# A graph network's sums over incoming edges: one product of 96 columns and one of 48 in place of three of 48

## The reference

```python
def _L0(x, w, b, src, dst, val):                  # sums to dst, once
    return relu(segment_sum(val[:, None] * (x @ w)[src], dst) + b)
def _L1(h, src, dst, ...):                        # sums to src, once
    msg = gate * h[dst] * (cw * mj)[:, None]
    agg = segment_sum(msg, src); tot = segment_sum(mj, src)
def _L2(x, w, src, dst):                          # twice
    x = segment_sum(x[src] * w[:, None], dst)
def _L3(x, src, dst, weight, bias):               # three times (Chebyshev, K = 4)
    prop = lambda h: segment_sum(w[:, None] * h[src], dst)
```

## Time and profile before

| | us |
|---|---|
| median of three runs | 18501.3 (18497.01 to 18546.9) |
| span of the profiled execution, first to last instruction | 16154.8 |
| what lies around the span, median less span | 2346.5 |
| seven stretches of the sums, together | 3718 |
| mean granted TensorE clock over the span | 0.809 |

### The profile page before, as it was taken

The page is one execution under the profiler, slowest core; times in us unless marked ns, Lnnn a source line. Parts: engine busy times, 40 slices in busy tenths (PEclk is TensorE's granted clock), DMA queues, the critical chain, the costliest instruction groups (busy, mean ns, idle before and its releaser), DMA issues. The chain is left out here.

```text
span 16154.8 us, 581780 instructions
## 1 busy us (share of the span) xinstructions
PE 10820.7 (67%) x194032; PEld 8866.5 (55%) x194033; DVE 12006.3 (74%) x25806; ACT 7455.3 (46%) x21241; POOL 7887.2 (49%) x7665
## 2 busy tenths in 40 slices
PE   5676767667610487867776677777766686676678
PEld 4555555555510366745555565656655565565556
DVE  9666766666633587789996888788777778777776
ACT  0111211112222366844456565766664474475466
POOL 0577777777767666013330077047307605713730
PEclk8777776776755699988888889998997797698789
DMA  8344433333367698979988698989779898988987
GB/s 341 111 124 124 124 120 124 124 122 123 123 167 186 177 371 308 321 261 342 331 298 257 231 350 295 304 310 350 272 252 385 317 313 334 369 281 310 386 288 237
DMA packets 1719187, 4103.16 MB, mean 254 GB/s; under 512 B 336706, under 2 KB 625440, under 8 KB 1718294
## 3 DMA queue, kind: packets, MB, share of 16 engines
q1 hardware_dynamic: 1287670, 3065.78, 57.5%
q0 software_dynamic: 431248, 1034.11, 16.6%
q10 hardware_dynamic: 144, 1.60, 0.0%
HBM read 2932.16 MB, written 1702.21 MB: 287 GB/s over the span
## 5 line engine op out<-in xcount | busy, mean ns | idle before, releaser
L1399 POOL DMA_INDIRECT messages<-exp_stage,exp_block_rows x3324 | 3569.8, 1074 | 4376.1 <-ACT exp_stage L1379 1827.6
L845 POOL DMA_INDIRECT records<-rec,row_i x3125 | 3116.6, 997 | 1442.7 <-issue 816.2
L1540 PEld LDWEIGHTS sum_sums<-sum_slots,sum_onehot 128*128 128x128 bf16 x93072 | 2522.1, 96 | 1138.7 <-issue 1131.8
L1540 PE MATMUL sum_sums<-sum_slots,sum_onehot 128*128 128x48 bf16 (+1 forms) x93072 | 2677.7, 183 | 637.5 <-DVE h L1466 507.1
L1497 ACT ACTIVATE sum_onehot<-iota_b,sum_late_places 128x128 bf16<-128x128 bf16 x5817 | 1910.2, 391 | 770.7 <-PE sum_sums L1540 687.8
L1257 PE MATMUL exp_rows<-tab,h 128*128 x39888 | 1806.2, 197 | 521.1 <-DVE h L1298 219.1
L1263 PE MATMUL exp_rows<-tab,h 128*128 x13296 | 1437.6, 284 | 923.5 <-ACT exp_stage L1379 668.0
L1257 PEld LDWEIGHTS exp_rows<-tab,h 128*128 128x128 bf16 x39888 | 1565.3, 102 | 876.5 <-issue 731.5
L1263 PEld LDWEIGHTS exp_rows<-tab,h 128*128 128x128 bf16 x13296 | 1222.1, 126 | 1138.7 <-issue 1106.5
L668 ACT COPY rec<-emeta 128x40 f32 (+1 forms) x625 | 140.2, 224 | 3070.9 <-DMA records<-rec,row_i 3070.9
L1298 DVE TENSOR_SCALAR h<-exp_places,pcol 128x2048 bf16<-128x2048 bf16 x1662 | 1271.9, 765 | 170.1 <-DMA exp_places<-src_places 146.5
(11 more groups left out here) (301 smaller groups left out, 22101.0 us busy)
## 6 DMA issues: line engine op xcount, KB each, us to landing
sum_slots<-messages SPq DMA_DIRECT2D x1662, 576.0 KB, 5.3
exp_places<-src_places SPq DMA_DIRECT2D x1662, 512.0 KB
sum_slots<-messages SPq DMA_DIRECT2D x277, 600.0 KB, 5.4
messages<-zeros SPq DMA_DIRECT2D x124, 1149.0 KB
l_places<-dst_places SPq DMA_DIRECT2D x277, 512.0 KB, 6.4
recc<-records SPq DMA_DIRECT2D x277, 448.0 KB, 4.7
l_gate<-records SPq DMA_DIRECT2D x277, 448.0 KB
records<-fill SPq DMA_DIRECT2D x215, 576.0 KB, 12.8
```

What stands on the lines that cost most here:

```text
L845: pool.indirect_dma_start(rec_dram, bass.IndirectOffsetOnAxis(ap=row_i[:, g, k:k + 1], axis=0), rec[:, g, k, :], None).then_inc(put[g], 16)
L1399: pool.indirect_dma_start(lines, bass.IndirectOffsetOnAxis(ap=row_d[:, c, g:g + 1], axis=0), stage[:, c, g, :], None, element_offset=0 if ...
L1540: last = pe.matmul(sums[:, c % RS, g, 0:width], onehot[:, c % RS, g * B + k, :], of[:, n * width:(n + 1) * width], start=n == 0, stop=n == ...
```

## The change

In `collect` each of the 16 one-hots of a chunk gets two products in place of three. The first has 96 columns, the first and second bf16 part side by side, and writes 96 columns of the sums; the second has 48, the third part, and accumulates onto columns 48 to 95. The sums are therefore kept as two halves in `parts`, 96 columns a window, and `finish` adds 96 columns. After the last chunk VectorE adds the two halves into `acc`. The zeroing covers twice the elements, one half on VectorE and one on GpSimd, with a semaphore `g_zero` that VectorE waits for ahead of its loop.

The rest finds room for `parts`: it shares the node table `tab` (`tab_f`, which is larger now) in five of the sums, and in the last three the places of `expand` and the one-hots of `collect` lie in the free end of `slots` (`tail`).

```diff
-        def collect(of_dram, rel, row, acc, width):
+        def collect(of_dram, rel, row, acc, width, room=None, onehot_room=None):
             length = B * 3 * width
+            wide = 2 * width
...
-                        c.step(dve.memset(acc_flat, 0.0))
+                        c.step(dve.memset(parts[:, 0:half_of_parts], 0.0))
                         keep(c)
+
+                    @block.gpsimd
+                    def _(pool):
+                        pool.memset(parts[:, half_of_parts:W * wide], 0.0).then_inc(g_zero, 1)
...
-                                to = acc_flat[:, bass.ds(ws[g] * width, width)]
+                                to = parts[:, bass.ds(ws[g] * wide, wide)]
...
-                                dve.tensor_tensor(to, to, sums[:, c % RS, g, 0:width], ALU.add).then_inc(g_acc, 1)
+                                dve.tensor_tensor(to, to, sums[:, c % RS, g, 0:wide], ALU.add).then_inc(g_acc, 1)
...
                         dve.wait_ge(g_iota, e + 1)
+                        dve.wait_ge(g_zero, e + 1)
                         turns_and_rest(dve, TURNS, REST, turn)
                         finish(LAST[0], False, LAST[1])
+                        dve.wait_ge(g_acc, (e + 1) * CHUNKS * CH)
+                        by_part = parts[:, 0:W * wide].rearrange("p (w j f) -> p w j f", j=2, f=width)
+                        dve.tensor_tensor(acc[:, :, :], by_part[:, :, 0, :], by_part[:, :, 1, :], ALU.add)
...
                                     for k in range(B):
-                                        for j in range(3):
-                                            n = k * 3 + j
-                                            last = pe.matmul(sums[:, c % RS, g, 0:width],
-                                                             onehot[:, c % RS, g * B + k, :],
-                                                             of[:, n * width:(n + 1) * width],
-                                                             start=n == 0, stop=n == 3 * B - 1)
+                                        at = k * 3 * width
+                                        pe.matmul(sums[:, c % RS, g, 0:wide], onehot[:, c % RS, g * B + k, :],
+                                                  of[:, at:at + wide], start=k == 0, stop=False)
+                                        last = pe.matmul(sums[:, c % RS, g, width:wide],
+                                                         onehot[:, c % RS, g * B + k, :],
+                                                         of[:, at + wide:at + 3 * width],
+                                                         start=False, stop=k == B - 1)
...
-            acc = scoped(s5, "acc1", [P, W, MSG], F32)
+            parts1 = scoped(s5, "parts1", [P, W, 2, MSG], F32)
+            acc = parts1[:, :, 0, :]
...
-        tab = sb("tab", [P, W, 3, D], BF16)
+        tab_f = sb("tab", [P, W * 2 * D])
+        tab = tab_f[:, 0:W * 3 * D // 2].bitcast(BF16).rearrange("p (w j f) -> p w j f", j=3, f=D)
+        tail = slots[:, W * D:2 * NS]
...
-            expand(tab, D, weighted)
-            collect(msg_dram, rel, win_d, acc, D)
+            room = None if weighted else tail
+            expand(tab, D, weighted, room)
+            collect(msg_dram, rel, win_d, acc, D, tab_f, room)
```

More of the change, by code:

```diff
@@ L1154, in split, with expand @@
             c.step(dve.tensor_copy(to[:, :, 2, :], rest))
-        def expand(table, width, weighted):
+        def expand(table, width, weighted, places_room=None):
             extra = width - D
@@ L1177, in expand @@
             with ExitStack() as s:
-                places = scoped(s, f"exp_places{e}", [P, RP, CH * B * P], BF16)
+                if places_room is not None:
+                    places = places_room[:, 0:RP * CH * B * P // 2].bitcast(BF16).rearrange("p (q n) -> p q n", q=RP)
+                else:
+                    places = scoped(s, f"exp_places{e}", [P, RP, CH * B * P], BF16)
                 onehot = h1_flat[:, 0:RS * CS * P // 2].bitcast(BF16).rearrange("p (q n e) -> p q n e", q=RS, e=P)
@@ L1408, in gnn_kernel @@
         g_load = sems("sum_load", RC)
-        g_oh, g_mm, g_acc, g_iota = (sem(f"sum_{n}") for n in ("onehot", "sums", "added", "iota"))
+        g_oh, g_mm, g_acc, g_iota, g_zero = (sem(f"sum_{n}") for n in ("onehot", "sums", "added", "iota", "zeroed"))
         g_rel, g_off, g_late = (sem(f"sum_{n}") for n in ("late_places", "distances", "late_onehots"))
@@ L1422, in collect @@
             in_order = of_dram.rearrange("(g p) f -> p g f", p=P)
-            acc_flat = acc[:, :, :].rearrange("p w f -> p (w f)")
             with ExitStack() as s:
+                parts = room if room is not None else scoped(s, f"sum_parts{e}", [P, W * wide], F32)
+                half_of_parts = W // 2 * wide
                 slots_in = scoped(s, f"sum_slots{e}", [P, RC, CH, length], BF16)
-                onehot = scoped(s, f"sum_onehot{e}", [P, RS, CS, P], BF16)
+                if onehot_room is not None:
+                    onehot = onehot_room[:, 0:RS * CS * P // 2].bitcast(BF16).rearrange(
+                        "p (q n e) -> p q n e", q=RS, e=P)
+                else:
+                    onehot = scoped(s, f"sum_onehot{e}", [P, RS, CS, P], BF16)
                 late_rel = scoped(s, f"sum_late_places{e}", [P, RC, NA], F32)
@@ L1910, in _ @@
                             dve.tensor_copy(srel[:, :, :, :], sent_in[:, :, 0:B].unsqueeze(3).to_broadcast([P, NG, B, 2]))
-                collect(back_dram, srel, win_s, acc, MSG)
+                collect(back_dram, srel, win_s, acc, MSG, parts1[:, :, :, :].rearrange("p w j f -> p (w j f)"))
             square = scoped(s5, "square1", [P, W, D], F32)
@@ L1936, in gnn_kernel @@
         acc = h1
-        tab = sb("tab", [P, W, 3, D], BF16)
+        tab_f = sb("tab", [P, W * 2 * D])
+        tab = tab_f[:, 0:W * 3 * D // 2].bitcast(BF16).rearrange("p (w j f) -> p w j f", j=3, f=D)
         third = 1.0 / 3.0
+        tail = slots[:, W * D:2 * NS]
+        assert 2 * NS - W * D >= RS * CS * P // 2
         def propagate(weighted, rel):
-            expand(tab, D, weighted)
-            collect(msg_dram, rel, win_d, acc, D)
+            room = None if weighted else tail
+            expand(tab, D, weighted, room)
+            collect(msg_dram, rel, win_d, acc, D, tab_f, room)
         with ExitStack() as s5:
@@ L1992, in gnn_kernel @@
         propagate(False, drel3)
-        t23 = sb("t23", [P, W, 2, D])
+        t23 = tab_f[:, :].rearrange("p (w k f) -> p w k f", k=2, f=D)
         def steps(node, c, dve):
@@ L2007, in gnn_kernel @@
                  (lambda w: t23[:, w, :, :].rearrange("p k f -> p (k f)"), cheb_sb[:, 1, :])], add_to_x,
-                tab[:, :, :, :].rearrange("p w j f -> p (w j f)")[:, 0:8 * PW * P].bitcast(F32).rearrange(
-                    "p (q k n) -> p q k n", q=2, k=2))
+                tail[:, 0:4 * PW * P].rearrange("p (q k n) -> p q k n", q=2, k=2))
         with nc.Block() as block:
```

## The result

The changed kernel is a little faster: 18442.07 us (median of 6 runs) against 18524.1 for the kernel before in the same session, ratio 0.9965 with a 95% interval of 0.9950 to 0.9981. The prediction was 18503 and no change. Its range held the time; the sign of the change it did not give.

A forecast was written before the change was run, and what follows sets the result against it. The prediction took a ring of waits between TensorE's products and VectorE's additions and one-hots in the sums as the bound. Ring -35, join +37 and zeroing 0 gave +2 us on the median 18501.3, so 18503; range 18410 to 18600.

The forecast's parts named there:

- The ring: In the sums, TensorE's product batch and VectorE's additions and one-hots wait for each other: 3.55 us per two chunks.
- the shift of 39: Allowance in the range for waits falling differently in the sums: 0.02 us a chunk on average, 39 us either way.
- Both are in the ring: VectorE's two additions per chunk, widened to 96 columns, each add 0.05 us: +0.10 us per two chunks.
- Products, -0.136 a link: TensorE's batch in the sums, with one 96-column product replacing two of 48, gets 0.136 us shorter per two chunks.
- The Trainium skill's formula: Warm product takes N / 2.4 + 2.5 ns; the batch would save only 0.04 us, giving 18596 us.
- VectorE's own work: In the sums, VectorE alone would need 1.56 us a chunk before the change, less than the measured chunk time.
- What lies around the span: Time outside the profile's 16154.8 us span, up to the runs' median of 18501.3: 2346.5 us, taken as unchanged.
- TensorE as the bound: Rival: TensorE bounds the sums, so every chunk gains 0.136 us, 264 less and 37 more: 18274 us; chance 0.06.
- The wide product that saves little: Rival: the 96-column product in the sums takes 45.4 to 50.8 ns, giving 18551 to 18634 us; chance 0.09.
- VectorE as the bound: Rival: VectorE's own instructions bound the sums, each chunk pays 0.10 us: +194 + 37, 18732 us; chance 0.05.
- the fallen clock: Rival: TensorE's clock falls to 1.2 GHz for a third of the sums: +230 us, 18733 us; chance 0.03.
- The rival of the ring at its favourable ends: In the sums, one addition hidden, wide product at 40 ns, or fewer instructions before TensorE's waits: about 18419 us; chance 0.13.

The follow-up runs named there:

- the opened ring: Kernel before, with VectorE adding the sums of two chunks before instead of one: ratio 0.9816 to the kernel before, sums 3362 us.
- the second's: The changed kernel measured again beside the variants, against the kernel before: ratio 0.9954 (0.9938 to 0.9970).

## Why the prediction was right or wrong

The kernel's bound was read rightly. The ring is shown by opening it: 3717 to 3362 us, with no operation made shorter. That the time lay in the range owes much to the range's width: it was 61 us under the forecast, and the forecast of no change failed. The range's lower end doesn't follow from its own recipe either, since 18419 less the shift of 39 is 18380 and not 18410.

The step that failed is "Both are in the ring (the second waits for the first, the one-hots stand behind both): +0.10 us a link". The term measured +0.05: the first addition's length counts (3584 to 3626 us when it alone is wide) and the second's does not (3584 to 3583). The row was there to be read: in the earlier trace rows the two additions begin at 6700.34 and take 0.55, to 6700.89, and the one-hots begin at 6700.86, before that end. The prediction named the case ("if the overlap with the next instruction hides one of them") and gave it 0.13 with the product at its favourable end. With +0.05 the sum is 970 x (-0.136 + 0.05) + 37 = -46 us.

The other terms:
- Products, -0.136 a link (132 us in all): right, 144 us between the changed kernel and its version with three products. The wide product goes every 41 to 42 ns in the trace of after, with the narrow behind it at 25 to 26 (42.3 and 25.4 in the prediction); from 7931.30 to 7931.37 a pair takes 0.07, and from the first start of the batch to its last (7932.36) it is 1.06, as forecast (1.058).
- The Trainium skill's formula, by which the saving would be 0.04 and the time 18596: the trace's 25.4 ns for 48 columns spoke against it. The section of the Trainium skill's page "TensorE: Matmul & The Clock Gate" that the prediction quotes ("Wait — 56ns, not 53.3ns?") also gives a floor of about 25 ns between starts, however few the columns, which the prediction left out. With that floor the page's figures make an estimate of 16 x (25 + 25 - 42.5) = 0.12 us a batch. The trace agrees with it (25.4).
- Join, +37: 5.06 us each (5.26 in the sum of width 50) with nothing beside them, and the next stage moves by as much when it is left out.
- Zeroing, 0: right, 4.02 us on GpSimd, ended before VectorE's.
- VectorE's own work, 1.56 us a chunk: 0.1 too long, as told above. It decided nothing in this change, but it made the expectations for the opened ring too high.
- What lies around the span, 2346.5 us: wrong, it is 2 us, and profile and runs were very probably of two chips. It moved neither the difference nor the range: both stand on the median of the runs, and the sums take the same on every chip here.

Of the rivals, TensorE as the bound is excluded by 144 us where it needed 264. The wide product that saves little is excluded by the batch of 1.24 us. VectorE as the bound and the fallen clock did not come.

The account: -84 to -87 in the sums and +35 for the join are about -50 us. The first ratio's interval is -93 to -35, and the second's -115 to -56, which leaves -50 out by a few microseconds. Both mix executions with the last stage at one clock or the other. Among those at the higher clock, by their times, the changed kernel is 62 us and 55 us under the kernel before; the 5 to 12 us that are left over -50 stay open. The rival of the ring at its favourable ends came half: the hidden addition did, the product at 40 ns did not.

## What to carry to other kernels

Where two engines wait for each other, find the ring, count how many chunks one link spans, and price an edit by what it adds to a link; and ask first whether the ring can span one chunk more, since here that was worth four times the change. For the last instruction ahead of a successor on the same engine, compare the starts in the timeline and not the durations: here the second addition could get 0.05 us longer at no cost, since the one-hots started before its end. Take what an engine needs for itself from rows in which nothing can hold it; here a wait of 0.1 us hid in such a row. An edit that shortens an engine inside a ring and lengthens its neighbour can change sign when the ring is opened, so measure it again after that.

## What the hardware showed beside it

In about half of the 1925 places of the sums VectorE started the one-hots 0.17 us after the start of the addition before them, whether that addition took 0.20 or 0.25 us; in a third it was 0.24, in the rest, at the turns above all, 0.5 and more, and these too were the same for both lengths. An addition that must see the previous one's result started 0.35 us after it at 48 columns and 0.40 at 96.

The last product stage (the f32 products with `cheb_sb` over 98 windows) ran mostly at 2.4 GHz (0.91 granted) or wholly at 1.2 GHz (0.50), from one execution to the next. Windows over it, the kernel before as the prediction had it and again:

```profile
16062.00:16139.00 77.00, 65.76 (x588) 65.63 (x588) 19.16 (x27) 26.21 (x50) 0.00 (x0) 0.91 0.00 1
```

```profile
16068.00:16200.00 132.00, 119.54 (x576) 117.80 (x576) 20.02 (x26) 26.24 (x50) 0.00 (x0) 0.50 0.00 0
```

That is some 55 us in 16200, with the same instructions. From the last addition to the end of the span it is 95 to 100 us in nine of the profiles kept and 152 to 157 in the other four, on all three chips. The times of the kernel before stand in two groups with it (18497 to 18501 and 18547 to 18551 in the first session, three each), while five of six runs of the changed kernel are in the lower one (18432 to 18455, and 18495). Lower against lower it is 18501 against 18439 in the median, 62 us, and in the second session 18508 against 18453, 55 us. Before that stage TensorE idles in both cases, behind VectorE's work on the nodes, so why the clock rose in one execution and not in the other stays open. Going by the times, 1 of 12 executions of the changed kernel was in the upper group and 9 of 17 of the kernel before in the same two sessions; whether the change has a part in that isn't shown.
